# The product with V cut in two along the queries, TensorE's attention program written out, maxima 24 tasks ahead

## The reference

```python
attn = jax.nn.softmax(jnp.einsum('bhqd,bhkd->bhqk', q, k) * scale, axis=-1)
out = jnp.einsum('bhqk,bhkd->bhqd', attn, v)
out = out.transpose(0, 2, 1, 3).reshape(B, T, C)
return out @ W_out + b_out
```

## Time and profile before

| | us |
|---|---|
| median of 3 runs | 1376.06 (1373.87 to 1379.99) |
| the profiled execution | 1376.95 |
| its span, first to last instruction | 1374.9 |
| PE busy | 1262.4 (92%) |
| DVE busy | 1035.0 (75%) |
| ACT busy | 751.8 (55%) |
| POOL busy | 538.0 (39%) |
| maxima on DVE, line 982 | 626.5 in 532 |
| exponentials on ACT, line 957 | 530.3 in 1024 |
| scores' matmuls on PE, line 1075 | 403.6 in 1024 |
| maximum matmuls on PE, line 1051 | 361.6 in 1064 |
| product with V on PE, line 1085 | 273.7 in 2048 records |

### The profile page before, as it was taken

One profiled execution on the slowest core, in us unless ns is written; L12 is line 12 of the kernel. 1 busy time (PEld: TensorE's weight loads), 2 busy tenths in 40 slices (PEclk: granted clock), 3 DMA queues, 4 the chain that ended last, 5 costly groups with the idle time before them and its releaser, 6 DMA issues. The chain is left out here.

```text
span 1374.9 us, 27467 instructions
## 1 busy us (share of the span) xinstructions
PE 1262.4 (92%) x6716; PEld 646.1 (47%) x6718; DVE 1035.0 (75%) x1653; ACT 751.8 (55%) x1616; POOL 538.0 (39%) x829
## 2 busy tenths in 40 slices
PE   5977848969899999999999999999899999989998
PEld 2543423323333333333333333333588888856665
DVE  6567768867788888888888888888455555538777
ACT  4534411756677777777777777777433333322221
POOL 6865734456422313131323222230267677730000
PEclk9998965997999999999999999999999999989999
DMA  5355414445333133322332133312454555547773
GB/s 189 126 146 176 142 46 143 175 125 170 108 86 83 50 89 95 74 71 63 97 81 74 55 96 87 79 54 61 147 159 156 159 158 157 160 169 220 239 237 125
DMA packets 126755, 169.25 MB, mean 123 GB/s; under 512 B 50109, under 2 KB 98653, under 8 KB 124702
## 3 DMA queue, kind: packets, MB, share of 16 engines
q1 hardware_dynamic: 111358, 126.79, 32.1%
q0 software_dynamic: 15360, 42.04, 9.3%
HBM read 96.58 MB, written 71.64 MB: 122 GB/s over the span
## 5 line engine op out<-in xcount | busy, mean ns | idle before, releaser
L982 DVE TENSOR_REDUCE mx<-pm 128x1 f32<-128x1024 f32 x532 | 626.5, 1219 | 88.4 <-PE pm L1051 88.3
L957 ACT ACTIVATE pr<-pst 128x512 f32<-128x512 f32 x1024 | 530.3, 603 | 212.8 <-PE pst L1075 211.9
L1075 PE MATMUL pst<-qt,kt 50*128 50x512 f32 x1024 | 403.6, 469 | 2.0 <-ACT pr L957 1.3
L1051 PE MATMUL pm<-kt,qt 48*128 48x512 f32 x1064 | 361.6, 451 | 20.4 <-DVE mx L982 15.3
L1051 PEld LDWEIGHTS pm<-kt,qt 48*128 48x128 f32 x1064 | 168.3, 193 | 271.1 <-DVE mx L982 239.5
L1085 PE MATMUL po<-pr,vt 128*17 128x512 f32 x2048 | 273.7, 607 | 0.7 <-ACT pr L957 0.7
L1075 PEld LDWEIGHTS pst<-qt,kt 50*128 50x128 f32 x1024 | 174.4, 187 | 86.3 <-ACT pr L957 79.3
L875 POOL CAST mp<-mx 128x16 fp32r<-128x16 f32 x33 | 6.5, 198 | 420.8 <-DVE mx L982 420.8
L1220 POOL DMA_INDIRECT s_y<-ys_c,slot_c x144 | 140.1, 973 | 79.2 <-issue 55.2
L1283 PE MATMUL c_pG<-w13s,xt_c 128*128 x576 | 150.4, 384 | 0.1
L897 POOL DMA_INDIRECT s_xg<-p_rows,p_slot x128 | 124.9, 976 | 56.5 <-issue 30.2
(11 more groups left out here) (197 smaller groups left out, 1335.3 us busy)
## 6 DMA issues: line engine op xcount, KB each, us to landing
xg<-s_xg SPq DMA_DIRECT2D x144, 128.5 KB
yg<-s_y SPq DMA_DIRECT2D x32, 512.0 KB, 4.3
kt<-s_k SPq DMA_DIRECT2D x34, 256.0 KB
qt<-s_q SPq DMA_DIRECT2D x68, 128.0 KB
s_q<-stg SPq DMA_DIRECT2D x32, 256.0 KB
s_k<-stg SPq DMA_DIRECT2D x32, 256.0 KB
vt<-s_v SPq DMA_DIRECT2D x17, 272.0 KB, 11.4
w13s<-w SPq DMA_DIRECT2D x1, 4608.0 KB
```

The costliest lines, as they stand in the source:

```text
L957: nc.scalar.activation(pr[:, (k % 2) * 4 + ORDER[i], :], pst[bank(gg, k, i)][:, :], ACT.Exp, scale=SCALE).then_inc(exp_ok, 1)
L982: nc.vector.tensor_reduce(mx[:, half, col:col + 1], pm[slot][:, :, :].rearrange("p a n -> p (a n)"), AX.X, ALU.max).then_inc(mx_free, 1)
L1051: mm = pe.matmul(pm[slot][:, kk, :], qt[buf][rows, half, pair, qi * P:(qi + 1) * P], kt[buf][rows, pair, kk * 512:(kk + 1) * 512], start=T ...
L1075: pe.matmul(pst[bank(buf, k, i)][:, :], kt[buf][rows, pair, kc * P:(kc + 1) * P], qt[buf][rows, half, pair, :], start=True, stop=True)\
```

## The change

`pv` gets a parameter `part` and does 256 of the 512 queries at a time. A quad on PE is now: two pairs (maximum and scores), the first half of the product of the quad before, two pairs, the second half. All four scores of a quad now lie within the quad itself. `pv_ok` counts two for each quad, and the waits for it are doubled. The order of heads (ORDER) is changed so that a pair still uses both halves of the rows. AHEAD is 24, so the prologue has four tasks more and SWITCH is 4: `turn_rows` stands at quads 4 and 12. `take_o` comes behind the fourth exponential of its quad, where it came behind the third. On PE all 16 groups are written out. The other engines keep their loops.

```diff
-AHEAD = 20
+AHEAD = 24
 SWITCH = (32 - AHEAD) // 2
 ROWS1, ROWS0 = SWITCH, SWITCH + 8
-ORDER = [2, 0, 1, 3]
+ORDER = [2, 3, 0, 1]
...
-                        need(act, pv_ok, q - 1)
+                        need(act, pv_ok, 2 * (q - 1))
...
-                            if k % 8 == 0 and i == 2:
+                            if k % 8 == 0 and i == 3:
...
-            def pv(buf, k, q, u):
-
-                pe.wait_ge(exp_ok, 4 * (q + 1))
-                if k % 8 == 0:
+            def pv(buf, k, q, u, part):
+
+                cols = slice(part * QH // 2, (part + 1) * QH // 2)
+                if part == 0:
+                    pe.wait_ge(exp_ok, 4 * (q + 1))
+                if k % 8 == 0 and part == 0:
                     need(pe, osb_ok, u)
                 for h in range(HG):
-                    mm = pe.matmul(po[32 * h:32 * h + VW, :], vt[buf][:, k % 8, h * VW:(h + 1) * VW],
-                                   pr[:, (k % 2) * 4 + h, :], start=(k % 8 == 0), stop=(k % 8 == 7),
+                    mm = pe.matmul(po[32 * h:32 * h + VW, cols], vt[buf][:, k % 8, h * VW:(h + 1) * VW],
+                                   pr[:, (k % 2) * 4 + h, cols], start=(k % 8 == 0 and part == 0), stop=(k % 8 == 7 and part == 1),
                                    tile_position=(0, 32 * h))
...
                                 max_half(mbuf, us[m], slots[m], place(g, k, m), kk)
-                                if m + kk:
-                                    if k % 8 == 0 and m + kk == 1:
-                                        pe.wait_ge(mrow_in[k // 8], 32 * (g + 1))
-                                    scores(gg, k, 2 * m + kk - 1, q)
-                                elif not (isinstance(q, int) and q == 0):
-                                    scores(gg if k else 1 - gg, (k - 1) % QUADS, 3, q - 1)
-                        if k == 1:
-                            pe.wait_ge(v_in[gg], 16 * (j + 1))
-                        if not (isinstance(q, int) and q == 0):
-                            pb, pk = (gg, k - 1) if k else (1 - gg, QUADS - 1)
-                            pv(pb, pk, q - 1, 2 * g + pk // 8 if k else 2 * g - 1)
+                                if k % 8 == 0 and m + kk == 0:
+                                    pe.wait_ge(mrow_in[k // 8], 32 * (g + 1))
+                                scores(gg, k, 2 * m + kk, q)
+                            if k == 1 and m == 0:
+                                pe.wait_ge(v_in[gg], 16 * (j + 1))
+                            if not (isinstance(q, int) and q == 0):
+                                pb, pk = (gg, k - 1) if k else (1 - gg, QUADS - 1)
+                                pv(pb, pk, q - 1, 2 * g + pk // 8 if k else 2 * g - 1, m)
...
-            rounds(pe, NG // 2, body)
-            scores(1, QUADS - 1, 3, NG * QUADS - 1)
-            pv(1, QUADS - 1, NG * QUADS - 1, 2 * NG - 1)
+            for j in range(NG // 2):
+                body(j)
+            for part in range(2):
+                pv(1, QUADS - 1, NG * QUADS - 1, 2 * NG - 1, part)
```

More of the change, by code:

```diff
@@ L823, in body @@
                         load(1 - gg, (g + 1) % NG)
-                        sp.wait_ge(pv_ok, g * QUADS)
+                        sp.wait_ge(pv_ok, 2 * g * QUADS)
                         load_v(1 - gg, (j + gg) % (NG // 2), 1 - gg)
@@ L964, in take_o @@
             def take_o(u):
-                act.wait_ge(pv_ok, 8 * (u + 1))
+                act.wait_ge(pv_ok, 16 * (u + 1))
                 nc.scalar.activation(osb[:, :], po[:, :], ACT.Copy).then_inc(osb_ok, 1)
```

## The result

The changed kernel takes 1398.41 us, median of 4 runs (1390.51 to 1402.09), where before took 1376.74 in the same comparison. The ratio is 1.0152, 95% interval 1.013 to 1.0173: 1.5% slower. The forecast was 1361 in a range of 1342 to 1388, so both the sign and the range were wrong. The profiled execution took 1402.09 us, its span 1400.3.

A forecast was written before the change was run, and what follows sets the result against it. A latency ring through ACT bound the quad at 2.60 us. Quads averaging 2.68 instead of 2.778 save 16.0, the head costs 0.5: 15.5 off 1376.95 gives 1361.4, median 1360.5, stated as 1361, range 1342 to 1388.

The forecast's parts named there:

- The ring: Before, each quad's latency loop through ACT and back, 2.60 us; claimed to vanish since all four scores end within the quad.
- Half product and block: PE's two parts of a half quad: half the product with V, 0.57 us, and two pairs, 0.65; quad 2.44.
- Rival (a): Switches between pairs and product on PE cost more than taken: 2.85 us a quad, 1399 us in all; chance 0.20.
- The special quads: Quads with `turn_rows` or `turn_out`, each using one `pm` buffer: 0.82 us more, twice in eight quads.
- The copy of `po`: The copy, now behind the fourth exponential, delays the product that overwrites `po`: 0.30 us once in eight quads.
- The head: Early stage B: four more prologue tasks and longer half clock, against some early gain, cost 0.5 us.
- POOL's chain: POOL's own indirect DMAs set the pace from 275 to 363 us; claimed to stay untouched, no change there.
- Costed at nothing: Items given no cost: DVE and ACT work, the next group's q and k (needed after 10.9 us), rows of `qt`.
- Rival (d): Next group's q and k come late at quad 4, by 1.5 us, 14 times: 21 more, 1382 us; chance 0.05.
- The written-out program: PE's program without its loop: no gain counted, at most 1.8 us from a 0.3 us hitch at six loop turns.
- (b): DVE becomes the bound: 2.58 us a plain quad, 2.77 over eight, 1381 us in all; chance 0.06.
- (c): PE's instructions, fetched once and never looped, come late: 0.3 us every five quads, 13 us, 1374 in all; chance 0.04.

## Why the prediction was wrong

- **The ring goes, PE is next, 2.44 us a quad: right.** Half product and block are 0.55 and 0.67 where I had 0.57 and 0.65. Rival (a), dearer switches, is out.
- **The special quads: right** (0.82 as put). The copy of `po` costs 0.38 where I had 0.30.
- **The head and POOL's chain: right.** PE goes on at 363.98 where I had 363.8. That it meets to 0.2 is luck: the same place lies at 361.84 with AHEAD = 22, at 370.26 with 20 and at 355.75 with the loads out.
- **The failed step is "Costed at nothing", the next group's q and k.** The need was right: 10.9 us after the group began. What I set against it was SP's issue ("the half needed first is issued by 663.7"), as if that were the landing. They land 12.5 us after the first issue. In the trace of before nothing waited for them, so no row gave their landing. But two things hinted at it. V's load, issued behind them (667.01), has its landing on the page of before (KB, median us from issue to landing):

```profile
vt<-s_v SPq DMA_DIRECT2D x17, 272.0 KB, 11.4
```

So a load on this queue could take that long, where the time from the issue of q's first half to its need was 6.0 us (663.7 to 669.7). And the windows of before show the transfers themselves (columns as in the earlier trace rows):

```profile
668.00:670.00 2.00, 2.00 (x16) 0.67 (x15) 1.70 (x3) 1.46 (x4) 0.00 (x0) 1.00 0.69 167
670.00:672.00 2.00, 2.00 (x15) 0.61 (x13) 2.00 (x2) 1.54 (x4) 0.00 (x0) 1.00 0.13 51
```

The DMA engines are busy until about 670, 11 us after the first issue at 658.79, V's 272 KB among it, and the need was put at 669.7. Rival (d) was this very wait, at 1.5 us and 14 times, a right size. I gave it 0.05 for "some 4 us" of cover that weren't there (by the prediction's own times it was 6.0, counted from the issue), and priced it at the wait alone. The half clock behind it brought nearly as much again (15 to 20 us beside 23). That is why the kernel is slower, where (d) at 1382 would still have been no clear change.
- **The written-out program**: I expected nothing to some 2 us, and it is worth 4 us in the kernel before and 78 with the short products. The hitch at the loop's turn, the only part of it that I had priced, stayed (2.90 us). The gain that I forecast needed it, and I had no term for it since I took the loop's cost from a body that fits.
- **(b), (c)** didn't come: DVE does 442 instructions in 500 us with the loads out, and fetching once costs nothing that shows.

The sum of the parts as the runs give them: before 1375.6, PE written out -4, AHEAD 22 +4, and short products in the new order about -15 give 1360.6; the last two tasks ahead give 1398.4. The -15 is what the others leave; no run has the new order alone.

## What to carry to other kernels

When a change shortens the time between a transfer's issue and its use, the issue isn't the time to set against the need. Look for the landing, of a neighbour on the same queue if nothing waits for the transfer itself, and price a missed deadline with the clock that it drags down. A number that sets how far ahead work runs has a deadline at either end: 20 was late for the rows of maxima, 24 for the loads, and 22 met both. Before a loop's body is made longer, see whether the instruction queue is silent while it turns, and look again in the longer one.

## What the runs showed of the hardware that I had not expected

- Waits of 1.1 to 2.2 us of an otherwise busy PE were followed by the half clock in 9 of 13 groups, and not by their length alone: one of 1.38 us was, one of 1.56 was not. Waits of 0.7 to 1.3 us, in the profiled execution of the kernel with the second half's loads later, were followed by it once in 13.
- A loop on PE turned without a fetch in the kernel before (no packet of that queue from 420 to 960 us), and with a body of a third more matmuls it was fetched at each turn and PE lost 8.1 to 9.4 us there (9.66 us between two half products where 1.22 is usual), with the next group's loads under way.
- Twelve loads with 1.5 MB took 12.4 to 13.2 us from the first issue until PE went on, which needs the first eight, and about half a microsecond of that was for the last four, which are issued after them.
